# Base rows stored from SP instead of ACT, and 125-row transfers cut into 112 and 13 rows

## The chip, the cores and the metric

The kernel runs on one core of a Trainium2 chip. The metric is the device time of one execution in microseconds, as the median of repeated runs. The profile is of one further execution; its instruction span starts at the first instruction and ends at the last.

## What is computed

The reference is two layers of a graph network over 1,250 nodes with 512 features: graph convolutions over 21,250 edges, linear attention, and expert layers. Only its two ends matter here. At the very start the input is normalised row by row. At the very end stands a feed-forward layer with a shared part and two banks of eight experts, in which each row goes to one expert of each bank:

```python
xn = _layernorm(x, axis=-1)          # start of layer 0
...
shared = gelu(x2 @ Ws1 + bs1) @ Ws2 + bs2
y = shared
y = y + _bank_residual(x2, Wr_sp, br_sp, W1_sp, b1_sp, W2_sp, b2_sp)
y = y + _bank_residual(x2, Wr_fq, br_fq, W1_fq, b1_fq, W2_fq, b2_fq)
```

`_bank_residual` picks the likeliest expert for each row, sends the row through that expert's two matrices with a gelu between them, and scales the result by the gate. The gelu and the second product are as in `shared`. The result is added to `x`.

## The kernel before

The 1,250 rows are held as 10 tiles of 125 rows (`TP`), one row on one partition. `GROUPS` are the tiles 0 to 3, 4 to 7, and 8 and 9. `R1t` and `R2t` are two SBUF buffers of [125, 10, 512] floats.

**Start.** SP loads the indices `dst` and `src`, then group 0 of the input (`load_x(0)`, 125 rows of 8 KB, L2800), the first weight unit (L2841) and groups 1 and 2. DVE first works out edge bounds (to L2454). Then `x_stats(0)` waits for group 0 and takes its statistics (L2465). On these depend the normalised rows, all later stages and the loading of the next weight unit.

**Last expert of layer 0** (in `stream_dve`, L1794 to L1806). DVE adds the results of tiles to `R2t` (`down`: L1462 is the addition, which frees a PSUM bank, L1420 the statistics) and splits transposed columns (`low_cols`, L1457). Products `q` of TensorE (L630 to L632) follow. They need the columns of their group and a free bank; the order of banks is that of the list `MIX`, eight in a ring.

**Routing and shared part of layer 1.** ACT normalises rows of the three groups (L1110), stores each group to the DRAM tensor `d_xg` (`store_rows`, L1351), and interleaves this with head rows (L1357). From `d_xg` rows are later gathered for each expert tile. The shared part ends in ten products (L1042 to L1047). DVE adds each to `R2t` (`add_shared`, L2141) and raises `base_ready`. These ten tiles are the base rows of the output. ACT stores them to `out` at the end of `stream_act`, one transfer of 125 rows of 2 KB for each tile (L1416), and each one waits for its tile.

**Expert tiles.** Rows are placed in 34 tiles of 128 slots (`NS` = 17 for each bank). For tile q POOL gathers rows from `d_xg` (`fetch_rows`, L2969), TensorE transposes them (`rows_to_cols`, L3023), ACT copies them (`turned`, L3096), TensorE makes the hidden layer (`hidden`, L3036), ACT applies the gelu (L3104), TensorE multiplies by the second matrix (`expert_out`, L3058), DVE scales (L3161) and copies the first matrix of the tile q + 3 out of the bank (`fetch_w1`, L3151), and POOL adds the rows to `out` (L2986, accumulating indirect transfer). TensorE goes round in this order: transposes of q + 2, hidden layer of q + 1, output of q. Before the first of them it makes `bias_columns` (L3046), which ACT copies (L3109).

ACT runs its program in order: L3109 and all `turned` and `gelu` copies stand behind the ten stores of L1416. POOL is in order too: it issues the gathers of tiles 0 to 6, waits until all base rows are stored (`out_stored`), adds tile 0, 1 and 2, gathers tile 7, adds tile 3, gathers tile 8, and so on. The gathers of tiles 4 and up wait for the transposes of the tile four before.

**Weights of the two banks.** SP loads each bank in four transfers of 2,048 KB (`load_bank`, L2848). Those of bank 1 are the second half: the first two wait for the last hidden product of the shared part, the other two for the last use of the shared weights. Bank 1 is first read for tile 17.

Of the kernel before, what the change touches and what calls it, by code (L numbers as in the profile page):

```python
# [19 lines left out]
TP = 125  # L20
NT = N // TP
# [96 lines left out]
PER = 10  # L118
EARLY = 4
LAST_TURN = [4, 5, 4]  # L120
COUNT_PARTS = [(0, 640), (640, 960), (960, 1120), (1120, 1200), (1200, 1240), (1240, N)]

LAST_U, LAST_D = f"u{E0 - 1}", f"d{E0 - 1}"
# [48 lines left out]
def program(nc, A, out):  # L172
    ctx = ExitStack()
    with ctx:
# [3 lines left out]
        def sem(name):  # L178
            return ctx.enter_context(nc.semaphore(name))


        d_xg = nc.dram_tensor("d_xg", [N, D], F32).ap()
# [49 lines left out]
        R1t = R1[0:TP, :].rearrange("p (t d) -> p t d", t=NT)  # L232
        R2t = R2[0:TP, :].rearrange("p (t d) -> p t d", t=NT)
# [219 lines left out]
        x_in = [sem(f"x_in{i}") for i in range(3)]  # L453
# [24 lines left out]
        out_stored = sem("out_stored")  # L478
# [69 lines left out]
        rows_stored = sem("rows_stored")  # L548
# [16 lines left out]
        base_ready = sem("base_ready")  # L565
# [9 lines left out]
        def rows_normed(eng, site, t):  # L575
            eng.wait_ge(normed_rows, NT * (site - (site > 1)) + t)
# [8 lines left out]
        def mx_bank(name):  # L585
            return ps[:, MJ[name] % 8, :]
# [5 lines left out]
        def mx_evacuated(eng, name):  # L592
            eng.wait_ge(mx_free[MJ[name] % 8], MJ[name] // 8 + 1)
# [4 lines left out]
        def stream_pe(pe, n, unit, unit_done):  # L598
# [128 lines left out]
            rows_unit("wr0")  # L727
            pe.wait_ge(counts_rounded, NT - 1 + len(COUNT_PARTS))
            pe.wait_ge(heavy_ready, 1)
# [338 lines left out]
        def stream_act(act):  # L1068
# [85 lines left out]
            for g in range(3):  # L1154
                root(1, g)
            for i in range(NT - 1 + len(COUNT_PARTS)):
                t = min(i, NT - 1)
                a, b = COUNT_PARTS[i - t] if t == NT - 1 else (0, N)
                if i:
                    act.wait_ge(counts_rounded, i)  # L1160
                act.activation(CTr[0:TP, t, a:b], CT[:, t, a:b], ACT.Copy).then_inc(counts_rounded, 1)
            for g in range(3):
                t0, t1 = GROUPS[g][0], GROUPS[g][-1] + 1
# [184 lines left out]
            def store_rows(g):  # L1348
                t0, t1 = GROUPS[g][0], GROUPS[g][-1] + 1
                rows_normed(act, 7, t1)  # L1350
                act.dma_start(d_xg.rearrange("(t p) d -> p t d", p=TP)[:, t0:t1, :], R1t[:, t0:t1, :])\  # L1351
                    .then_inc(rows_stored, 16)

            def head_rows(*tiles):
                for t in tiles:
# [46 lines left out]
            for i in range(6):  # L1402
# [8 lines left out]
                    .then_inc(mx_sem(("su", i)), 1)  # L1411
                mx_evacuated(act, ("su", i))
                act.activation(HH[:, i % 2, c0:c0 + w], V[:, i % 4, 0:w], ACT.Copy).then_inc(shared_high, 1)
            for t in range(NT):
                act.wait_ge(base_ready, t + 1)
                act.dma_start(out[TP * t:TP * t + TP, :], R2t[:, t, :]).then_inc(out_stored, 16)  # L1416

        def stream_dve(dve, n, own, settle, row, heads, per_head, fetch_w1):
            def stats(src, t):
# [33 lines left out]
            def low_cols(site, name, ts):  # L1453
                for t in ts:
                    s = slice(TP * t, TP * t + TP)
                    dve.wait_ge(cols_high, NT * site + t + 1)
                    dve.tensor_tensor(XL[:, :, s], mx_bank((name, t))[:, 0:TP * KC].rearrange("p (k e) -> p k e", k=KC),  # L1457
                                      XH[:, :, s].bitcast(F32), ALU.subtract).then_inc(mx_sem((name, t)), 1)
# [288 lines left out]
            for e in range(E0):  # L1747
                def gelu_low(i):
                    c0, w = CH[i // 2]
                    v0, v1 = V[:, 2 * (i % 2), 0:w], V[:, 2 * (i % 2) + 1, 0:w]  # L1750
                    dve.wait_ge(gelu_ready, 12 * e + 2 * i + 2)
                    dve.tensor_tensor(v0, v0, v1, ALU.add).then_inc(gelu_summed, 1)
                    dve.wait_ge(hidden_high, 6 + 6 * e + i + 1)
                    dve.tensor_tensor(HL[:, i % 2, c0:c0 + w], v0, HH[:, i % 2, c0:c0 + w].bitcast(F32), ALU.subtract)\
                        .then_inc(hidden_low, 1)

                def up(i):
                    c0, w = CH[i // 2]
                    o = mx_wait(dve, (f"u{e}", i))
                    if e == 0:  # L1760
                        mx_evacuated(dve, ("wb", 2 * (i // 2) + 1))
                        mx_evacuated(dve, ("wb", 2 * (i // 2)))
                    dve.wait_ge(hidden_low, 6 + 6 * e + i - 1)
                    own(dve.tensor_tensor(V[:, 2 * (i % 2), 0:w], o[:, 0:w], BC[:, 0, c0:c0 + w], ALU.mult))
                    dve.tensor_tensor(V[:, 2 * (i % 2) + 1, 0:w], o[:, 0:w], BC[:, 1, c0:c0 + w], ALU.mult)\
                        .then_inc(mx_sem((f"u{e}", i)), 1)

                def down(some):
                    for t in some:
                        if e:  # L1770
                            mx_evacuated(dve, (f"d{e - 1}", t))
                        add_row((f"d{e}", t), R2t[:, t, :], R2t[:, t, :])
                        if e == E0 - 1:
                            mx_evacuated(dve, (f"d{e}", t))
                            stats(R2t[:, t, :], t)

                up(0)
                for i in range(1, 4):
                    up(i)
                    gelu_low(i - 1)  # L1780
                if e == E0 - 1:
                    gelu_low(3)
                    down(GROUPS[0])
                    spreads(0)
                    up(4)
                else:
                    up(4)
                    gelu_low(3)
                up(5)
                gelu_low(4)  # L1790
                gelu_low(5)
                if e < E0 - 1:
                    down(range(NT))
                else:  # L1794
                    scales(5, 0)
                    down(range(4, 6))
                    low_cols(5, "t6", GROUPS[0])
                    down(range(6, 8))
                    spreads(1)
                    down(range(8, 9))  # L1800
                    scales(5, 1)
                    down(range(9, 10))
                    spreads(2)
                    scales(5, 2)
                    low_cols(5, "t6", GROUPS[1])
                    low_cols(5, "t6", GROUPS[2])  # L1806
# [292 lines left out]
            for i, (c0, w) in enumerate(CH):  # L2099
                dve.wait_ge(shared_high, 4 + i)  # L2100
                dve.tensor_tensor(mT[PARTS:2 * PARTS, c0:c0 + w], mx_bank(("mt", i))[PARTS:2 * PARTS, 0:w],
                                  mT[PARTS:2 * PARTS, c0:c0 + w].bitcast(F32), ALU.subtract).then_inc(mx_sem(("mt", i)), 1)
            dve.wait_ge(rows_stored, 48)
            own(dve.tensor_scalar(tile_i, sloti[0:TP, :], 7, None, ALU.logical_shift_right))
            settle()
            own(dve.tensor_copy(tile_f, tile_i))
# [62 lines left out]
        def graph_pe(pe, n, unit, unit_done, v4):  # L2169
# [177 lines left out]
            for i in range(3):  # L2347
                turn_part(NG - 1, i, LAST_TURN[i])

        def graph_dve(dve, n, own, settle, row):  # L2350
# [109 lines left out]
                dve.tensor_tensor(wL[unit_slot(u)], wraw, wH[unit_slot(u)].bitcast(F32), ALU.subtract).then_inc(w_ready, 1)  # L2460

            def x_stats(g):
                dve.wait_ge(x_in[g], 16)
                for t in GROUPS[g]:
                    own(dve.bn_stats(bnst[0:TP, 6 * t:6 * t + 6], R1t[:, t, :]))  # L2465

# [118 lines left out]
            for b in range(NB):  # L2585
# [16 lines left out]
                if b - 1 in IN_LOOP:  # L2602
                    kind, t = IN_LOOP[b - 1]
# [53 lines left out]
        def graph_act(act, n):  # L2657
# [134 lines left out]
            for i in range(3):  # L2792
                store_turned(NG - 1, i, LAST_TURN[i])


        @block.sync
        def _(sp):
            def load_x(g):
                t0, t1 = GROUPS[g][0], GROUPS[g][-1] + 1
                sp.dma_start(R1t[:, t0:t1, :], A["x"][:, t0:t1, :]).then_inc(x_in[g], 16)  # L2800

            sp.dma_start(V[0:TP, 1, 0:NCH].bitcast(I32), A["dst"]).then_inc(edges_loaded, 16)
            sp.dma_start(V[0:TP, 0, 0:NCH].bitcast(I32), A["src"]).then_inc(edges_loaded, 16)
# [42 lines left out]
            def load_bank(g, e):  # L2846
                u = len(UNITS) + E * g + e
                sp.dma_start(wbank[g][:, UNIT * e:UNIT * e + 2 * UNIT].rearrange("p (e w) -> p e w", e=2),  # L2848
                             A["units"][u:u + 2].rearrange("e p w -> p e w")).then_inc(bank_loaded[g], 16)
# [5 lines left out]
            load_bank(0, 4)  # L2855
            sp.wait_ge(w_used, len(UNITS) - 1)
            load_bank(0, 6)
            sp.wait_ge(mx_full, MJ[("su", 5)] + 1)
            for e in (0, 2):
                load_bank(1, e)  # L2860
# [5 lines left out]
        def _(pool):  # L2866
# [50 lines left out]
            for u in range(EARLY, len(UNITS)):  # L2917
# [13 lines left out]
                if u == 4:  # L2931
                    pool.wait_ge(zeroed, 16)
                    pool.wait_ge(heavy_idx_ready, 1)
                    for t in range(NT):
                        pool.indirect_dma_start(
                            out=d_heavy, out_offset=bass.IndirectOffsetOnAxis(ap=heavy_idx[:, t:t + 1], axis=0),
# [34 lines left out]
                    in_offset=bass.IndirectOffsetOnAxis(ap=backi[:, q:q + 1], axis=0), bounds_check=N - 1, oob_is_err=False)\  # L2971
                    .then_inc(row_loaded[q % 4], 16)

            pool.wait_ge(rows_stored, 48)
            for q in range(4):
                fetch_rows(q)
            for q in range(2 * NS):
                if q == NS:
                    for i in range(3):
                        pool.wait_ge(y_added[i], 16 * len(range(i, NS, 3)))  # L2980
                for f in range(4, 7) if q == 0 else range(q + 4, min(q + 5, 2 * NS)) if q >= 3 else ():
                    fetch_rows(f)
                if q == 0:
                    pool.wait_ge(out_stored, 16 * NT)
                pool.wait_ge(y_ready, q + 1)
                pool.indirect_dma_start(  # L2986
                    out=out, out_offset=bass.IndirectOffsetOnAxis(ap=backi[:, q:q + 1], axis=0),
                    in_=ysb[q % 3], in_offset=None, bounds_check=N - 1, oob_is_err=False, compute_op=ALU.add)\
                    .then_inc(y_added[q % 3], 16)
# [243 lines left out]
```

## Time and profile before

| | |
|---|---|
| median of 3 runs | 1701.74 us (1699.98 to 1703.64) |
| profiled execution | 1704.72 us |
| its span of instructions | 1703.0 us |
| mean granted TensorE clock | 0.969 of full speed |
| TensorE busy | 1554.8 us (91%) |
| VectorE (DVE) busy | 989.0 us (58%) |
| ScalarE (ACT) busy | 445.3 us (26%) |
| GpSimd (POOL) busy | 305.7 us (18%) |

Busy time is that in which an engine carries out an instruction; waits and the issuing of transfers don't count in it. An engine name with a q (ACTq, SPq, POOLq, DVEq) is the queue or sequencer of this engine: there an issue of a transfer shows. The profiled execution lies 3.0 us above the median, and 1.7 us of it lie around the span.

### The profile page before, as it was taken

How to read it: one execution, taken by the hardware profiler on the slowest of the kernel's cores; microseconds unless marked ns; L12 is line 12 of the kernel's file. 1: busy time of each engine (PE TensorE's matmuls, PEld its weight loads, DVE VectorE, ACT ScalarE, POOL GpSimd, SP SyncE). 2: the span in 40 equal slices, each digit the busy share in tenths (PEclk: the TensorE clock that was granted, in tenths of full speed). 3: DMA queues.
4: the chain of work that ended last, by engine and by line, in shares of the span. 5: the costliest groups of instructions: out<-in, count | busy, mean ns of one | idle time of the engine just before them, and what ended most of it. 6: DMA issues, size and time to landing. Idle time of an engine off the chain costs nothing.

```text
span 1703.0 us, 23777 instructions
## 1 busy us (share of the span) xinstructions
PE 1554.8 (91%) x8983; PEld 1215.1 (71%) x8983; DVE 989.0 (58%) x1767; ACT 445.3 (26%) x854; POOL 305.7 (18%) x191
## 2 busy tenths in 40 slices
PE   3798887797999999999998999998999999896998
PEld 3677777786777777877786788877767755575765
DVE  6877778789954672386256666765254512762332
ACT  3422111123311220130124242434224101441222
POOL 1000002044111031004001212122111100002665
PEclk9899998999999999999998999999999999897999
DMA  4122224341221010012001010100101321545443
GB/s 148 49 66 88 96 94 151 128 149 63 86 92 49 1 66 28 1 49 68 25 1 50 25 50 26 50 26 25 50 25 51 115 87 68 222 166 186 67 80 45
DMA packets 51754, 123.93 MB, mean 73 GB/s; under 512 B 8033, under 2 KB 28408, under 8 KB 44510
## 3 DMA queue, kind: packets, MB, share of 16 engines
q1 hardware_dynamic: 12414, 62.78, 10.4%
q10 hardware_dynamic: 29375, 49.37, 8.3%
q0 software_dynamic: 9856, 10.28, 3.6%
q8 instruction: 74, 1.21, 0.3%
q14 instruction: 35, 0.29, 0.0%
HBM read 92.87 MB, written 40.22 MB: 78 GB/s over the span
## 4 chain that ended last, share of the span: by engine, by line
PE 75%; DVE 10%; DMA 7%; ACT 3%; issue 3%; ACTq 1%; POOL 1%; DVEq 0%; SPq 0%; POOLq 0%
PE ps L619 9%; PE ps L620 9%; PE ps L621 9%; PE ps L2284 5%; PE ps L677 4%; PE ps L679 4%; PE ps L630 4%; PE ps L631 4%; PE ps L632 4%; PE ps L938 3%; DMA arena<-d_kv 3%; PE ps L3036 3%; PE ps L3058 3%; PE ps L825 2%; DMA arena<-d_w 2%
## 5 line engine op out<-in xcount | busy, mean ns | idle before, releaser
L619 PE MATMUL ps<-wslot,XH 128*125 128x512 f32 (+2 forms) x560 | 215.0, 384 | 5.6 <-DVE XL L1457 3.9
L620 PE MATMUL ps<-wslot,XH 128*125 128x512 f32 (+2 forms) x560 | 212.9, 380 | 0.0
L621 PE MATMUL ps<-wslot,XL 128*125 128x512 f32 (+2 forms) x560 | 212.5, 380 | 0.0
L2927 POOL CAST wslot<-arena 128x2048 fp32r<-128x2048 f32 x25 | 47.7, 1907 | 798.2 <-PEq L3004 428.5
L630 PE MATMUL ps<-XH,wslot 128*128 128x500 f32 (+1 forms) x336 | 123.2, 367 | 16.2 <-DVE XL L1457 6.2
L1462 DVE TENSOR_TENSOR arena<-ps,arena 125x512 f32<-125x512 f32 x150 | 98.3, 684 | 50.5 <-PE ps L621 45.5
L619 PEld LDWEIGHTS ps<-wslot,XH 128*125 128x125 f32 x560 | 104.7, 187 | 31.4 <-issue 4.5
L677 PE MATMUL ps<-CTr,Hhi 125*128 125x500 f32 (+1 forms) x360 | 125.0, 361 | 0.0
L631 PE MATMUL ps<-XH,wslot 128*128 128x500 f32 (+1 forms) x336 | 121.6, 362 | 0.0
L621 PEld LDWEIGHTS ps<-wslot,XL 128*125 128x125 f32 x560 | 104.7, 187 | 22.8
L632 PE MATMUL ps<-XL,wslot 128*128 128x500 f32 (+1 forms) x336 | 120.8, 360 | 0.0
L620 PEld LDWEIGHTS ps<-wslot,XH 128*125 128x125 f32 x560 | 104.7, 187 | 21.9 <-issue 0.2
L2284 PE MATMUL ps<-arena 125*128 x1330 | 95.9, 228 | 26.2 <-DVE arena L2558 22.4
L2929 POOL TENSOR_TENSOR wslot<-arena,wslot 128x2048 fp32r<-128x2048 f32 x25 | 117.1, 4684 | 2.0
L679 PE MATMUL ps<-CTr,Hlo_head 125*128 125x500 f32 (+1 forms) x324 | 109.8, 352 | 0.0
L2284 PEld LDWEIGHTS ps<-arena 125*128 125x128 bf16 x1330 | 83.2, 102 | 33.7 <-issue 33.5
L2558 DVE TENSOR_SCALAR arena<-arena 125x1280 bf16<-125x1280 int16 x133 | 72.5, 570 | 47.0 <-PE ps L2284 46.3
L630 PEld LDWEIGHTS ps<-XH,wslot 128*128 128x128 f32 x336 | 65.7, 195 | 30.4 <-issue 17.3
L938 PE MATMUL ps<-arena 125*128 125x500 f32 (+1 forms) x240 | 84.6, 513 | 1.3 <-DMA arena<-d_w 1.3
L1511 DVE TENSOR_TENSOR V<-ps,BC 128x500 f32<-128x500 f32 (+1 forms) x36 | 21.3, 592 | 107.4 <-PE ps L683 106.6
L3036 PE MATMUL ps<-V,arena 128*128 128x128 f32 x544 | 69.5, 283 | 14.9 <-ACT V L3096 13.8
L677 PEld LDWEIGHTS ps<-CTr,Hhi 125*128 125x128 f32 x360 | 67.8, 188 | 15.1 <-issue 5.6
(445 smaller groups left out, 3062.6 us busy)
## 6 DMA issues: line engine op xcount, KB each, us to landing
arena<-in_units SPq DMA_DIRECT2D x29, 1024.0 KB, 4.8
arena<-in_units SPq DMA_DIRECT2D x8, 2048.0 KB, 11.1
d_w<-arena ACTq DMA_DIRECT2D x10, 625.0 KB
d_wt<-arena ACTq DMA_DIRECT2D x10, 625.0 KB, 3.5
rows<-in_rows ACTq DMA_DIRECT2D x22, 256.0 KB, 4.2
d_kv<-V SPq DMA_DIRECT2D x20, 250.0 KB
arena<-d_kv SPq DMA_DIRECT2D x20, 250.0 KB
arena<-d_wt ACTq DMA_DIRECT2D x2, 2441.4 KB
```

What stands on the lines that cost most here:

```text
L619: pe.matmul(o, lhsT=xh[:, k, s], rhs=H4[:, k, 0:nw], start=k == 0, stop=False, skip_group_check=True)
L620: pe.matmul(o, lhsT=xh[:, k, s], rhs=L4[:, k, 0:nw], start=False, stop=False, skip_group_check=True)
L621: last = pe.matmul(o, lhsT=xl[:, k, s], rhs=H4[:, k, 0:nw], start=False, stop=k == K - 1, skip_group_check=True)
L630: pe.matmul(o, lhsT=H4[:, k, f], rhs=XH[:, k, c0:c0 + w], start=k == 0, stop=False, skip_group_check=True)
L631: pe.matmul(o, lhsT=L4[:, k, f], rhs=XH[:, k, c0:c0 + w], start=False, stop=False, skip_group_check=True)
L632: last = pe.matmul(o, lhsT=H4[:, k, f], rhs=XL[:, k, c0:c0 + w], start=False, stop=k == KC - 1, skip_group_check=True)
L677: pe.matmul(o, lhsT=Hhi[0:TP, t, f], rhs=CTr[0:TP, t, c0:c0 + w], start=t == 0, stop=False, skip_group_check=True)
L679: pe.matmul(o, lhsT=Hlo[t][0:TP, f], rhs=CTr[0:TP, t, c0:c0 + w], start=False, stop=False, skip_group_check=True)
L938: last = pe.matmul(o, lhsT=src[:, t, 128 * m:128 * m + 128], rhs=slab_of(i)[:, t, 0:w], start=t == 0, stop=t == NT - 1, skip_group_check=True)
L2284: last = pe.matmul(ps[:, 3 * (b % 2) + t // 4, 128 * (t % 4):128 * (t % 4) + 128], lhsT=buffer[:, 128 * t:128 * t + 128], rhs=pre_flat[:, ...
L2929: pool.tensor_tensor(wL[unit_slot(u)], wraw, wH[unit_slot(u)].bitcast(F32), ALU.subtract).then_inc(w_ready, 1)
L3036: last = pe.matmul(ps[:, 2 + q % 2, ST * m:ST * m + ST], lhsT=w1_of[q][:, k // 2, FF * (k % 2) + 128 * m:FF * (k % 2) + 128 * m + 128], rh ...
```

## The change

The ten stores of base rows leave ACT's program. SP issues them, behind its loads of bank 0 and ahead of those of bank 1. Each transfer of 125 rows among the input loads, the stores to `d_xg` and the base rows becomes two, of rows 0 to 111 and 112 to 124, and the waits count twice as much. In the last expert of layer 0 the additions of tiles 6 and 7 stand ahead of `low_cols` of group 0 and their statistics behind it.

```diff
+ROW_PARTS = ((0, 112), (112, TP))
...
             def store_rows(g):
                 t0, t1 = GROUPS[g][0], GROUPS[g][-1] + 1
                 rows_normed(act, 7, t1)
-                act.dma_start(d_xg.rearrange("(t p) d -> p t d", p=TP)[:, t0:t1, :], R1t[:, t0:t1, :])\
-                    .then_inc(rows_stored, 16)
+                for a, b in ROW_PARTS:
+                    act.dma_start(d_xg.rearrange("(t p) d -> p t d", p=TP)[a:b, t0:t1, :], R1t[a:b, t0:t1, :])\
+                        .then_inc(rows_stored, 16)
...
-            for t in range(NT):
-                act.wait_ge(base_ready, t + 1)
-                act.dma_start(out[TP * t:TP * t + TP, :], R2t[:, t, :]).then_inc(out_stored, 16)
...
                     scales(5, 0)
                     down(range(4, 6))
+                    for t in (6, 7):
+                        mx_evacuated(dve, (f"d{e - 1}", t))
+                        add_row((f"d{e}", t), R2t[:, t, :], R2t[:, t, :])
                     low_cols(5, "t6", GROUPS[0])
-                    down(range(6, 8))
+                    for t in (6, 7):
+                        mx_evacuated(dve, (f"d{e}", t))
+                        stats(R2t[:, t, :], t)
                     spreads(1)
...
-            dve.wait_ge(rows_stored, 48)
+            dve.wait_ge(rows_stored, 96)
...
-                dve.wait_ge(x_in[g], 16)
+                dve.wait_ge(x_in[g], 32)
...
-                sp.dma_start(R1t[:, t0:t1, :], A["x"][:, t0:t1, :]).then_inc(x_in[g], 16)
+                for a, b in ROW_PARTS:
+                    sp.dma_start(R1t[a:b, t0:t1, :], A["x"][a:b, t0:t1, :]).then_inc(x_in[g], 16)
...
             load_bank(0, 6)
+            for t in range(NT):
+                sp.wait_ge(base_ready, t + 1)
+                for a, b in ROW_PARTS:
+                    sp.dma_start(out[TP * t + a:TP * t + b, :], R2t[a:b, t, :]).then_inc(out_stored, 16)
             sp.wait_ge(mx_full, MJ[("su", 5)] + 1)
             for e in (0, 2):
                 load_bank(1, e)
...
-            pool.wait_ge(rows_stored, 48)
+            pool.wait_ge(rows_stored, 96)
...
-                    pool.wait_ge(out_stored, 16 * NT)
+                    pool.wait_ge(out_stored, 32 * NT)
```

## Rows read from the trace of the kernel before

**Rows 1.** The page: the chain that ended last, by engine.

```profile
PE 75%; DVE 10%; DMA 7%; ACT 3%; issue 3%; ACTq 1%; POOL 1%; DVEq 0%; SPq 0%; POOLq 0%
```

**Rows 2.** The chain from 1537 to 1563 us: start us, us, what.

```profile
1539.15 9.21 ACTq L1416
...
1548.41 4.54 ACTq L1416
...
1553.76 3.78 PE ps L3036 x16
1557.55 0.85 PE ps L3023 x4
1558.40 2.42 PE ps L3036 x16
1560.82 1.72 PE ps L3058 x4
```

**Rows 3.** ACT's timeline, 1515 to 1555 us: start us, us, instruction [idle before].

```profile
1517.14 0.41 ACT L1413 ACTIVATE HH<-V 128x250 fp32r<-128x250 f32 x1
1523.87 29.08 ACTq L1416 DMA_DIRECT2D out<-arena  x10
1553.00 0.23 ACT L3109 ACTIVATE V<-ps 128x68 f32<-128x68 f32 x1 [35.44 <-issue]
```

**Rows 4.** TensorE's timeline ahead of its stop, 1539 to 1542 us.

```profile
1539.27 0.92 PE L3046 MATMUL ps<-BC,rows 8*128 8x17 f32 x7 [1.97 <-issue]
...
1540.24 1.09 PE L3023 MATMUL ps<-ident,rows 128*128 128x128 f32 x8
```

**Rows 5.** The chain some tiles later, at full clock.

```profile
1591.61 0.44 PE ps L3023 x4
1592.19 2.02 PE ps L3036 x16
...
1596.37 1.79 PE ps L3036 x16
```

**Rows 6.** Windows: busy of PE, PEld, DVE, ACT, POOL, granted clock, DMA share, GB/s.

```profile
1153.00:1157.00 4.00, 4.00 (x12) 3.20 (x12) 3.71 (x12) 0.30 (x1) 0.75 (x1) 0.57 0.54 176
1534.00:1538.00 4.00, 3.30 (x15) 2.32 (x13) 1.59 (x3) 0.00 (x0) 0.00 (x0) 1.00 0.32 126
1544.00:1548.00 4.00, 0.00 (x0) 0.00 (x0) 0.00 (x0) 0.00 (x0) 0.00 (x0) 0.50 1.02 422
```

**Rows 7.** The gather of tile 4, and the time to landing of all 34 gathers.

```profile
1541.66 1.00 POOL L2969 DMA_INDIRECT rows<-d_xg,BC  x1 [10.80 <-PE ps L3023]
...
DMA to landing us min/median/max: 2.9/3.9/8.1
```

**Rows 8.** The chain at the gather of tile 7.

```profile
1574.32 4.31 DMA rows<-d_xg,BC
```

**Rows 9.** SP's issues of bank loads (L2848) in ns, and their time to landing.

```profile
L2848 SPq DMA_DIRECT2D arena<-in_units x8: 367/376/480, 1449.6 to 1537.8; - x8
...
DMA to landing us min/median/max: 7.3/11.1/17.2
```

**Rows 10.** DVE's timeline at the start; the second row is of 0 to 28 us.

```profile
11.07 0.69 DVE L2454 TENSOR_SCALAR BC<-BC 128x40 f32<-128x40 f32 x4
15.02 2.47 DVE L2465 BATCH_NORM_STATS2 small<-arena 125x6 f32<-125x512 f32 x4 [3.25 <-DMA arena<-in_x]
```

**Rows 11.** The chain at ACT's stores of normalised rows.

```profile
1476.50 0.26 ACTq L1351
1476.76 0.33 issue
...
1486.78 0.26 ACTq L1351
```

**Rows 12.** DVE's timeline in the last expert of layer 0.

```profile
1149.63 2.43 DVE L1457 TENSOR_TENSOR XL<-ps,XH 128x500 fp32r<-128x500 f32 x4 [0.57 <-ACT XH L1083]
1151.98 0.68 DVE L1462 TENSOR_TENSOR arena<-ps,arena 125x512 f32<-125x512 f32 x1
```

**Rows 13.** TensorE's timeline at the first product that follows.

```profile
1152.81 0.46 PE L630 MATMUL ps<-XH,wslot 128*128 128x500 f32 x1 [2.98 <-DVE arena L1462]
```

**Rows 14.** DVE's timeline: the copy of tile 17's first matrix, the first use of bank 1.

```profile
1621.66 0.69 DVE L3151 COPY arena<-arena 128x1024 f32 x1 [0.63 <-issue]
```

## The prediction

> **What bounds the kernel now.** I read the page first. The reader is to see there that the chain which ended last is three quarters TensorE and has only 1% in ACTq, ACT's issuing of transfers [rows 1]. An average over 1,700 us hides where that 1% lies, so I followed the chain through each place that the diff touches.
>
> At the end of the shared part the chain leaves TensorE altogether. It stands on L1416, ACT's stores of base rows, from 1539.15 to 1552.95 us, 9.21 and 4.54 us for two issues [rows 2]. ACT's own timeline shows the same from the other side: its last copy ends at 1517.6, the ten issues stretch over 29.08 us, and the next activation, L3109, comes at 1553.00 after 35.44 us without work [rows 3]. TensorE has done the bias columns and the transposes of two tiles by 1541.33 [rows 4] and then waits for ACT's copy until 1553.76. The last base row is ready when the chain enters ACTq at 1539.15, so what comes behind is the issuing itself. The windows say why an issue takes that long. From 1534 to 1538 us, with only the 125-row stores under way, the DMA share is 0.32 at 126 GB/s, while bank loads of 128 rows reach 1.02 and 422 GB/s in 1544 to 1548 [rows 6]. A 125-row transfer thus occupies five of the sixteen DMA engines. On these five the stores stand behind 4 MB of bank loads, and ACT's issues are held up when too much is outstanding. That last link is inferred from the order of events; the stall is measured.
>
> **The stores move to SP.** ACT loses ten issues, and L3109 stands directly behind a copy that ends at 1517.6. The next thing that is late is TensorE itself. Its bias columns and transposes don't move: they follow the last base addition. They end at 1540.24 + 1.09 = 1541.33 [rows 4]. ACT's copy of the first tile runs beside the second tile's transposes, so the hidden layer of tile 0 can start at about 1541.5 instead of 1553.76. Behind that point the before needed 3.78 + 0.85 + 2.42 + 1.72 and small gaps, to 1562.54 [rows 2]. It had half the clock (0.50 in the window ahead [rows 6]) because TensorE had stood still. Without the stop these are 2.02 + 0.44 + 1.79 + 1.72 = 5.97 [rows 2, 5], so with 0.1 of gaps the output of tile 0 is full at 1547.6. That is 14.9 us earlier: 12.3 of wait and 2.6 of clock. Bounds: 12.3 if the clock falls as before, 15.0 if nothing else holds.
>
> SP gets twenty issues of at most 0.48 us [rows 9], two for each tile. An addition takes 0.68 us [rows 12], so SP may lag by one or two tiles, but the last ones wait for TensorE; it is through by about 1540.3. The DMA engines are empty at this time. At 422 GB/s a tile's 256 KB takes 0.6 us, and the fastest bank load landed 7.3 us after issue for 5.0 us of data at that rate, which leaves 2.3 us beside the data. All base rows are stored by about 1543.5, and POOL first asks for them when tile 0 is scaled, at about 1549. That wait costs nothing.
>
> What is queued behind the stores on SP are the four bank 1 loads. The first two start near 1540.5 instead of 1516.6. 8.39 MB plus some 1.5 MB of gathers and additions at 422 GB/s last until about 1564. Their first use is the copy for tile 17 at 1621.66 [rows 14], which moves to about 1608; 44 us of cover are left. The collision is elsewhere: gathers now run beside them. Beside bank loads a gather took up to 8.1 us, against a median of 3.9 [rows 7]. Tile 4's is issued at 1541.66 and lands by 1549.8, needed when tile 1's output is made, 1547.6 + 3.95 = 1551.6. Tiles 5 and 6 have more room. Tile 7's is issued behind POOL's addition of tile 2 and is on the chain already before, with 4.31 us at 1574.32 [rows 8]. Moved up by 14.9 it lies at 1559.4 to 1563.7, inside the loads. It then takes between 4.3 and 8.1 us, so it costs 0 to 3.8 us; I take the middle, 2.0. Later gathers find the queues empty. Net of this part: -14.9 + 2.0 = -12.9 us.
>
> **Input in 112 and 13 rows.** DVE is free at 11.76 and waits 3.25 us for group 0 of the input [rows 10]. Its 1,024,000 bytes take 8.1 us at 126 GB/s and 2.4 us at 422 [rows 6]. 112 rows divide over sixteen engines, and the remaining 13 rows are 106 KB. If the rate rises, the input lands at about 9.4 and the wait is gone: -3.25 us, which cannot be more since DVE's bounds come first. DVE's work behind it is the chain, so it carries on. The lower bound is 0. One issue more on SP ahead of the weight unit costs 0.4 us on a unit that isn't awaited before the statistics are done. In the Trainium skill, "DMA: Bandwidth & Descriptors", section "Why a DMA increments its semaphore by 16 and not by 1", the number of engines is the largest one up to 16 that divides the outer dimension: 5 for 125 rows, 16 for 112, 13 for 13. By that rule the trace agrees for 125 (0.32 is 5 of 16), and no row here shows the other two.
>
> **Normalised rows in two parts.** ACT issues three transfers more. An issue takes 0.26 and the next activation starts 0.30 to 0.59 after it [rows 11]. The first two are on the chain and the third nearly. I take 0.8 us, with bounds of 0.3 and 1.8. Their quicker landing wins nothing: DVE doesn't wait for `rows_stored` behind the routing.
>
> **The additions of tiles 6 and 7.** TensorE's first product starts at 1152.81, after the addition of tile 6, which starts at 1151.98 and lasts 0.68 [rows 12, 13]. With both additions first, DVE uses its 0.57 us of idle time, but `low_cols` starts some 0.7 us later and ends near 1152.75 instead of 1152.06, and the product needs that too. 0 us, with 0.5 either way.
>
> **Sum.** -12.9 - 3.25 + 0.8 = -15.35 us. The profiled execution took 1704.72, so its like would take 1689.4. It is 3.0 above the median of the runs. From the median, 1701.74 - 15.35 = 1686.4 us.
>
> **The rivals.**
> - *The clock falls all the same.* Between 1537 and 1541.5 TensorE has only small products and one pause of 1.97 us [rows 4]. After a pause of 2.98 us [rows 13] it got 0.57 of the clock for 4 us [rows 6], so 0.43 x 4 = 1.7 us were lost. Here: 1688.1. For it, the low use; against it, a shorter pause.
> - *Cutting transfers doesn't spread them.* The input still arrives at 15.0, and the base rows need about 20 us on five engines, until near 1546, still in time. 1686.4 + 3.25 = 1689.6. For it there is no row; against it, that 128-row loads use all engines. The Trainium skill, same page, section "Rules for kernel authors", says of two transfers to disjoint partition halves not to bother, since both go over the same engines; by that rule the result is this rival, but it speaks of a tile that divides evenly.
> - *Contention holds more than one gather.* If tiles 4 to 8 or the additions' landings each come late, I count two further delays of 3 us: 1692.4. Against it, POOL's slack of several us on tiles 5 and 6.
> - *ACT is not what holds tile 0.* Then only start and issues remain: -3.25 + 0.8, 1699.3, within 0.2%. Against it, gathers 0 to 3 and bank 0 have landed before 1541.
> - *Bank 1 comes too late* and the kernel is slower. Place: the copy for tile 17 at 1608. Each us of landing behind it costs one. It decides at 1608 + 15.35 = 1623, when the loads run below about 100 GB/s; at 90 GB/s they end near 1634 and the time is 1712. Against it stands 422 GB/s.
>
> **How the numbers follow.** The forecast has a chance of 0.60, the clock 0.17, no spreading 0.08, more contention 0.08, ACT not the cause 0.04, bank 1 0.03. Bounds of the forecast: tile 7's gather 2.0 less or 1.8 more, issues 0.5 less or 1.0 more, the reorder 0.5: 1683.4 to 1689.7. With the clock, the missing spread and the scatter of the runs (1.9) the range is 1682.5 to 1692. 0.2% (3.4 us) is about what this measurement can tell from no change. Faster by more than that: 0.60 + 0.17 + 0.08 + 0.08 = 0.93; same 0.04; slower 0.03.
>
> **What would show it.** L3109 directly behind `bias_columns`, near 1538 (with the start's shift); no pause of TensorE over 2 us between shared part and tile 0; clock 1.0 there; L2465 without a wait on `in_x`; a DMA share above 0.9 while the input loads; gather 7 landing in more than 4.3 us; bank 1 landing near 1562. I am wrong if TensorE's stop only finds another releaser, or if the 3.25 us come back as a wait between 20 and 80 us.

## The result, and the profile after

The changed kernel took 1696.09 us (median of 13 runs, 1691.34 to 1701.31) against 1703.68 us (13 runs, 1698.98 to 1710.93) for the kernel before: ratio 0.9952, 95% interval 0.9939 to 0.9966. It is faster, by 8 us where 15 were forecast, and its time lies above the predicted range. A later comparison gave 0.9959 (0.9942 to 0.9975). The ratios here and below are not the plain quotients of the medians; they differ from them by up to 0.0014. Single runs of one kernel spread over 10 us. The profiled execution took 1692.29 us, so the stages are compared below, not the ends.

The chain after, in the order of time (start us, us, what), over the stretch that answers to [rows 2] and [rows 8]:

```profile
1535.83 3.53 PE ps L3045 x16
1539.36 0.59 PE ps L3032 x4
1539.95 1.79 PE ps L3045 x16
1541.74 1.72 PE ps L3067 x4
...
1554.77 10.13 DMA rows<-d_xg,BC
1564.94 1.11 PE ps L3032 x4
1566.06 3.62 PE ps L3045 x16
1569.68 2.07 PE ps L3067 x4
```

ACTq is gone from it. In its place stands a wait that was 4.31 us before: the gather of tile 7, now 10.13 us. What follows runs slowly: 1.11, 3.62 and 2.07 us for the transposes, the hidden layer and the output product, which take 0.44, 1.79 and 1.72 at full clock.

ACT's timeline after, and below it SP's, which answer to [rows 3]:

```profile
1512.10 0.41 ACT L1415 ACTIVATE HH<-V 128x250 fp32r<-128x250 f32 x1
1534.59 0.23 ACT L3118 ACTIVATE V<-ps 128x68 f32<-128x68 f32 x1 [22.08 <-PE ps L3055]
```

```profile
1518.82 15.69 SPq L2866 DMA_DIRECT2D out<-arena  x20
1534.55 3.42 SPq L2853 DMA_DIRECT2D arena<-in_units  x4
```

ACT no longer waits in its queue but for TensorE's bias columns (L3055), and SP issues the four loads of bank 1 together, behind the last base row.

TensorE's timeline after:

```profile
1564.94 1.11 PE L3032 MATMUL ps<-ident,rows 128*128 128x128 f32 x4 [5.72 <-DMA rows<-d_xg,BC]
```

Windows after (columns as in [rows 6]):

```profile
1536.00:1540.00 4.00, 4.00 (x22) 4.00 (x23) 0.49 (x1) 0.81 (x4) 2.36 (x2) 0.57 0.89 330
1548.00:1552.00 4.00, 4.00 (x27) 3.00 (x26) 1.49 (x3) 1.28 (x4) 1.59 (x1) 1.00 1.00 400
1560.00:1564.00 4.00, 0.00 (x0) 0.00 (x0) 1.45 (x2) 0.00 (x0) 2.78 (x3) 0.93 1.02 280
1564.00:1568.00 4.00, 3.06 (x14) 2.82 (x15) 0.00 (x0) 0.60 (x1) 0.97 (x1) 0.50 0.81 165
```

The DMA engines are full until 1564. The granted clock falls twice: to a mean of 0.57 in the window of the hidden layer of tile 0, and to 0.50 after the stop at tile 7.

DVE's timeline at the start, which answers to [rows 10]:

```profile
11.17 0.69 DVE L2458 TENSOR_SCALAR BC<-BC 128x40 f32<-128x40 f32 x4
12.05 2.47 DVE L2469 BATCH_NORM_STATS2 small<-arena 125x6 f32<-125x512 f32 x4 [0.19 <-DMA arena<-in_x]
```

The wait for the input fell from 3.25 to 0.19 us.

Stages of each profiled execution, in us. A: start of the input statistics. B: from the first store of normalised rows to the transposes of the logits (the scores by which a row's expert is picked). C: from the first bias column to the first output product of tile 0. D: from there to the end. A, B and C are starts, or differences of starts, in the traces; D is the span less the start of that output product.

| kernel | A | B | C | D |
|---|---|---|---|---|
| before | 15.0 | 21.4 | 21.3 | 142.5 |
| after | 12.0 | 22.4 | 8.0 | 149.1 |
| change, second profile (d4) | 12.0 | 24.2 | 7.6 | 149.7 |
| a1, bank 1 left out | 12.0 | 22.4 | 7.9 | 143.4 |
| a2, half of bank 1 first | 12.1 | 24.0 | 7.7 | 142.1 |
| a3, gathers early | 11.9 | 22.9 | 8.0 | 141.0 |
| a4, bank 1 late | 13.3 | 23.9 | 7.6 | 152.1 |
| b1, input alone | 12.0 | 21.4 | 21.4 | 142.8 |
| b2, move alone | 15.2 | 21.3 | 6.3 | 152.9 |
| b3, cut stores on ACT | 15.0 | 21.3 | 7.5 | 143.4 |
| c1, a2 and a3 | 11.9 | 22.6 | 7.9 | 135.7 |
| d1, all on ACT, gathers early | 11.9 | 21.4 | 6.3 | 135.7 |
| d2, gathers early alone | 15.1 | 21.3 | 21.2 | 135.6 |
| d3, c1 with two parts undone | 11.9 | 21.4 | 6.4 | 135.7 |

### The profile page after: what moved, and what is told of

The parts are those of the page before. It is cut to its first block, busy times and chain, and to the rows that moved or that the text cites. A ratio compares the mean times of both kernels' runs of the same rounds, so it can differ in the third digit from the quotient of the medians.

```text
span 1690.6 us, 23793 instructions
## 1 busy us (share of the span) xinstructions
PE 1555.0 (92%) x8983; PEld 1214.2 (72%) x8983; DVE 989.6 (59%) x1767; ACT 445.7 (26%) x854; POOL 305.1 (18%) x191
## 4 chain that ended last, share of the span: by engine, by line
PE 75%; DVE 11%; DMA 5%; issue 3%; ACT 3%; POOL 1%; PEld 0%; DVEq 0%; ACTq 0%; PEldq 0%; SPq 0%; POOLq 0%
PE ps L620 9%; PE ps L621 9%; PE ps L622 9%; PE ps L2288 6%; PE ps L678 4%; PE ps L680 4%; PE ps L631 4%; PE ps L632 4%; PE ps L633 4%; PE ps L939 3%; PE ps L3045 3%; PE ps L3067 3%; PE ps L826 2%; DMA d_w<-arena 2%; DMA arena<-d_w 2%
## 5 line engine op out<-in xcount | busy, mean ns | idle before, releaser
L1510 DVE TENSOR_TENSOR V<-ps,BC 128x500 f32<-128x500 f32 (+1 forms) x36 | 21.3, 592 | 107.3 <-PE ps L684 106.6
L678 PEld LDWEIGHTS ps<-CTr,Hhi 125*128 125x128 f32 x360 | 67.8, 188 | 15.1 <-issue 5.6
L1129 ACT ACTIVATE V<-V,cols 128x500 f32<-128x500 f32 (+1 forms) x96 | 56.0, 631 | 85.1 <-DVE V L1764 85.1
```

Source lines behind the costliest of these rows:

```text
L678: pe.matmul(o, lhsT=Hhi[0:TP, t, f], rhs=CTr[0:TP, t, c0:c0 + w], start=t == 0, stop=False, skip_group_check=True)
```

## The experiments

The theory after the result: the loads of bank 1, late and all together, hold the gather of tile 7. It is tested by taking the loads away, moving them, and giving the gather more time.

**a1: bank 1 is not loaded**, and tiles 17 to 33 take bank 0's weights, so the second bank's weights are left out of the computation.

```diff
-            sp.wait_ge(mx_full, MJ[("su", 5)] + 1)
-            for e in (0, 2):
-                load_bank(1, e)
-            sp.wait_ge(w_used, len(UNITS))
-            for e in (4, 6):
-                load_bank(1, e)
...
```

> The changed kernel without the four loads of bank 1; tiles 17 to 33 take bank 0's weights instead, so the second bank's weights are left out. Theory (contention): tile 7's gather took 10.1 us beside these loads and stopped TensorE for 5.7 us, after which the clock was at half for a while. Without them it lands in about 4.3 us, TensorE waits under 1 us, and some 7 us are saved against the changed kernel: ratio to the kernel before 0.991, against 0.995 for the change itself. Rival A (the gather is late for another reason, such as the additions to rows that were just stored): TensorE still waits 5 us at tile 7, ratio 0.995. Rival B (the missing gain was lost before the expert tiles): tile 7 no longer waits, but the time hardly moves.

Measured: 1688.88 us, ratio 0.9923 (0.9897 to 0.9949). TensorE waited 2.1 us in all for gathers instead of 7.1, and D fell from 149.1 to 143.4. The loads are the cause of the late gather; rivals A and B fall.

**a2: the first two loads stand ahead of the base rows again.**

```diff
+            sp.wait_ge(mx_full, MJ[("su", 5)] + 1)
+            for e in (0, 2):
+                load_bank(1, e)
             for t in range(NT):
                 sp.wait_ge(base_ready, t + 1)
...
-            sp.wait_ge(mx_full, MJ[("su", 5)] + 1)
-            for e in (0, 2):
-                load_bank(1, e)
             sp.wait_ge(w_used, len(UNITS))
```

> The changed kernel with the first two loads of bank 1 ahead of the base rows on SP, as they were before the change; the other two behind. Theory (contention): 4 MB of the 8 are through before the shared part ends, the rest by about 12 us after its end, and tile 7's gather (some 21 us after it) finds empty queues: it lands in 4 to 5 us, TensorE waits under 1 us, ratio to before 0.991. The base rows stand behind 4 MB on SP's queue, but they are asked for only 12 us after the last of them. Rival A: the wait of 5 us at tile 7 stays, ratio 0.995. Rival C (base rows behind bank loads are late again): the addition of tile 0 waits for them, ratio above 0.995.

Measured: 1688.67 us, ratio 0.9902 (0.9877 to 0.9927). TensorE's waits for gathers sum to 0.6 us and D is 142.1, against 142.5 before the change. The whole loss in D came from the place of 4 MB of loads.

**a3: each gather from tile 7 on one addition earlier.**

```diff
-                for f in range(4, 7) if q == 0 else range(q + 4, min(q + 5, 2 * NS)) if q >= 3 else ():
+                for f in range(4, 7) if q == 0 else range(q + 5, min(q + 6, 2 * NS)) if q >= 2 else ():
```

> The changed kernel with each gather from tile 7 on issued one addition earlier (tile q + 5 ahead of the addition of tile q). Theory (contention, and no slack of the gathers): tile 7's is issued about 4 us earlier, still beside the loads, takes 8 to 10 us and stops TensorE for 1 to 2 us instead of 5.7; the small waits of later tiles (7.5 us in all by the trace after) vanish as well. Ratio to before 0.991 to 0.992. Rival A': POOL is the bound in the tiles and order makes no difference, ratio 0.995.

Measured: 1687.04 us, ratio 0.9903 (0.9878 to 0.9927), a little better than expected, though the stop itself was priced too low. The gather of tile 7 took longer still, 11.43 us where 8 to 10 were expected, and it had only the additions of tiles 0 and 1 ahead of it. The chain of a3:

```profile
1552.38 11.43 DMA rows<-d_xg,BC
```

TensorE stops for 3.2 us at this tile instead of 1 to 2, and never again for a gather: D is 141.0 with this stop in it.

**a4: bank 1 held back until six tiles are scaled.**

```diff
+            sp.wait_ge(y_ready, 6)
             sp.wait_ge(mx_full, MJ[("su", 5)] + 1)
```

> The changed kernel with all four loads of bank 1 held back until tile 5 is scaled. Theory (contention, any gather has next to no slack): tile 7's gather lands in about 4 us, but one issued beside the loads, of tile 10 or later, takes 8 to 10 us and stops TensorE for 4 to 6 us; ratio 0.994 to 0.995, as the change itself. Rival A (it is special to the first additions): no tile waits over 2 us, ratio 0.991.

Measured: 1699.1 us, ratio 0.998 (0.9965 to 0.9995), slower than the change itself. SP's issue and TensorE's stop, from the two timelines of a4:

```profile
1568.42 2.11 SPq L2853 DMA_DIRECT2D arena<-in_units  x4
```

```profile
1580.56 1.11 PE L3033 MATMUL ps<-ident,rows 128*128 128x128 f32 x4 [5.14 <-DMA rows<-d_xg,BC]
```

The stop moved with the loads, from tile 7 to tile 10, whose gather is the first one issued after them and takes 9.33 us (at 1571.18). D grew to 152.1, which is 3.0 more than in the change and more than expected. Another 1.3 us are lost at the start: in this trace alone of those with the cut input, the statistics begin at 13.3 instead of 12.0. So tile 7 is not special. The gather of tile 12 takes about 13.1 us (from 1579.04), but TensorE stands for it only 0.7 us: after one long stop the next gathers have slack.

The next four take the change apart.

**b1: the input loads alone.**

```diff
...
-                sp.dma_start(R1t[:, t0:t1, :], A["x"][:, t0:t1, :]).then_inc(x_in[g], 16)
+                for a, b in ((0, 112), (112, TP)):
+                    sp.dma_start(R1t[a:b, t0:t1, :], A["x"][a:b, t0:t1, :]).then_inc(x_in[g], 16)
```

> The kernel before with the input loads alone in 112 and 13 rows. Theory: DVE's wait of 3.25 us for group 0 of the input falls to 0.2 us as in the trace after, and all later work moves up by 3.0 us: ratio 0.998. Rival (the start's gain is given back by a later wait): DVE's wait is gone but the time doesn't move, ratio 1.000.

Measured: 1699.79 us, ratio 0.9983 (0.9968 to 0.9998), and A fell from 15.0 to 12.0. The time is as expected, so the gain at the start is carried to the end, though the interval only just excludes no gain at all.

**b2: the stores on SP, uncut.**

```diff
-            for t in range(NT):
-                act.wait_ge(base_ready, t + 1)
-                act.dma_start(out[TP * t:TP * t + TP, :], R2t[:, t, :]).then_inc(out_stored, 16)
...
+            for t in range(NT):
+                sp.wait_ge(base_ready, t + 1)
+                sp.dma_start(out[TP * t:TP * t + TP, :], R2t[:, t, :]).then_inc(out_stored, 16)
             sp.wait_ge(mx_full, MJ[("su", 5)] + 1)
```

> The kernel before with the base rows stored from SP at the new place, but each in one transfer of 125 rows, and nothing else changed. Theory: ACT is free, so TensorE's stop of 12.4 us ahead of tile 0 goes, as in the change. The ten stores need some 20 us on five engines and all four loads of bank 1 stand behind them on these engines, so they land later than in the change and hold tile 7's gather at least as long (over 5 us of wait): ratio 0.996 to 0.998. Rival (the cut into 112 and 13 rows is what helps at this place): TensorE still stops over 5 us before tile 0 or at the addition of tile 0.

Measured: 1699.22 us, ratio 0.9975 (0.9957 to 0.9994). C fell by 15.0 us, and D rose by 10.4. The queue and the stop, from the timelines of b2:

```profile
1537.09 7.75 SPq L2845 DMA_DIRECT2D arena<-in_units  x4
```

```profile
1550.56 1.64 POOL L2986 DMA_INDIRECT out<-arena,BC  x1 [7.97 <-DMA out<-arena]
...
1556.26 1.08 POOL L2969 DMA_INDIRECT rows<-d_xg,BC  x1 [0.30 <-issue]
```

```profile
1569.65 1.11 PE L3023 MATMUL ps<-ident,rows 128*128 128x128 f32 x4 [9.56 <-DMA rows<-d_xg,BC]
```

The slow stores hold SP's four issues of the loads for 7.75 us, and POOL's first addition waits until the stores have landed. The next two follow at once, so the gather of tile 7 is issued 20.2 us after the first bias column, no later than in the change (21.3). But it lands about 13.4 us later, where the change has 10.13, and stops TensorE for 9.56 us. So beside the move the cut saves 3 to 4 us of D. ACT is freed here without any cut: C is 6.3.

**b3: the stores cut, still on ACT.**

```diff
             for t in range(NT):
                 act.wait_ge(base_ready, t + 1)
-                act.dma_start(out[TP * t:TP * t + TP, :], R2t[:, t, :]).then_inc(out_stored, 16)
+                for a, b in ((0, 112), (112, TP)):
+                    act.dma_start(out[TP * t + a:TP * t + b, :], R2t[a:b, t, :]).then_inc(out_stored, 16)
...
```

> The kernel before with the base rows still stored by ACT, at the old place, but in transfers of 112 and 13 rows; nothing on SP moves. Theory: ACT was held because its 125-row stores pile up on five engines; over sixteen they are through in under 1 us each, the last issue ends about 1 us after the last base row, and TensorE's stop shrinks from 12.4 us to under 2. The loads of bank 1 keep their old place, so tile 7's gather isn't late: some 12 us are won, ratio 0.992 to 0.993, more than by the change itself. Rival (an issue from ACT is slow because it competes with SP's bank loads, whatever its shape): the stalls of 10 and 4.5 us in ACT's queue remain, ratio 0.998 to 1.000.

Measured: 1691.13 us, ratio 0.9911 (0.9886 to 0.9936). This is the run that tells most. ACT's timeline in b3:

```profile
1529.10 15.71 ACTq L1417 DMA_DIRECT2D out<-arena  x20
1545.03 0.23 ACT L3110 ACTIVATE V<-ps 128x68 f32<-128x68 f32 x1 [22.29 <-PE ps L3047]
```

The issues themselves, in ns (shortest, median, longest), before and in b3:

```profile
L1416 ACTq DMA_DIRECT2D out<-arena x10: 268/566/9972, 1523.9 to 1548.4; - x10
```

```profile
L1417 ACTq DMA_DIRECT2D out<-arena x20: 327/410/937, 1529.1 to 1544.3; - x20
```

Twenty issues take 15.71 us, the time in which the base rows come, where ten took 29.08 [rows 3]. None takes over 0.94 us, where the longest took 9.97. ACT's next activation waits for TensorE and not for the queue. The loads keep their old place, so D is 143.4. The cut alone, without a new engine, gives more than the whole change: what held ACT was the shape of the transfer, and b2 shows the same shape holding SP. An issue from ACT beside SP's bank loads is not slow in itself.

**c1: a2 and a3 together.**

```diff
+            sp.wait_ge(mx_full, MJ[("su", 5)] + 1)
+            for e in (0, 2):
+                load_bank(1, e)
             for t in range(NT):
                 sp.wait_ge(base_ready, t + 1)
...
-                for f in range(4, 7) if q == 0 else range(q + 4, min(q + 5, 2 * NS)) if q >= 3 else ():
+                for f in range(4, 7) if q == 0 else range(q + 5, min(q + 6, 2 * NS)) if q >= 2 else ():
```

> The changed kernel with both edits that won 8 us each: the first two loads of bank 1 ahead of the base rows, and the gathers one addition earlier. Theory: both take away the same wait, so they don't add: about 1 us more than either, from the small waits of later tiles; ratio 0.989 to 0.990. Rival (they take away different waits): 0.986 or less.

Measured: 1680.3 us, ratio 0.9854 (0.9829 to 0.9878). My theory that both take away the same wait falls; the rival's 0.986 is met. Windows of TensorE (busy, clock, DMA share, GB/s), before and in c1:

```profile
1600.00:1640.00 40.00, 38.29 (x236) 1.00 0.34 59
```

```profile
1600.00:1640.00 40.00, 40.00 (x243) 1.00 0.46 85
```

Far from any bank load the kernel before leaves TensorE idle for 1.7 us in 40. With early gathers it is never idle. D is 135.7, which is close to 34 rounds of 3.95 us (134.3).

**d2: early gathers on the kernel before** (the edit of a3 alone).

```diff
-                for f in range(4, 7) if q == 0 else range(q + 4, min(q + 5, 2 * NS)) if q >= 3 else ():
+                for f in range(4, 7) if q == 0 else range(q + 5, min(q + 6, 2 * NS)) if q >= 2 else ():
```

> The kernel before with the gathers one addition earlier and nothing else. Theory: without contention too, each gather has no slack, and small waits make 34 tiles take 142.5 us from the first output on where the two edits together took 135.7; the order of gathers alone gives 6 us of that: ratio 0.996 to 0.997, with ACT's stop of 13.75 us unchanged. Rival (the early gather only helps when it meets bank loads): tile stage as before, ratio 1.000.

Measured: 1697.9 us, ratio 0.9959 (0.994 to 0.9977), C as before and D 135.6. So the order of gathers has a gain of 6.9 us of its own in D.

**d1: input cut, base rows cut but on ACT, early gathers** (the edits of b1, b3 and a3 on the kernel before; the one of the base rows is shown).

```diff
...
-                act.dma_start(out[TP * t:TP * t + TP, :], R2t[:, t, :]).then_inc(out_stored, 16)
+                for a, b in ((0, 112), (112, TP)):
+                    act.dma_start(out[TP * t + a:TP * t + b, :], R2t[a:b, t, :]).then_inc(out_stored, 16)
...
```

> The kernel before with three edits that each won alone: input loads in 112 and 13 rows, base rows in 112 and 13 rows but still from ACT, gathers one addition earlier. SP's order, the stores of normalised rows and DVE's order stay as before. Theory: the base rows' shape is what freed ACT, their engine is of no matter, and the three gains are of three places and add: 15 + 3 + 6 us, ratio 0.985 to 0.986, as with the stores on SP behind half of bank 1. Rival (ACT's twenty issues cost time that SP's don't): 0.988 or more.

Measured: 1677.51 us, ratio 0.986 (0.9831 to 0.9889). The gains add as expected.

**d3: c1 without the cut of the normalised rows and with the old order of additions** (against c1; the stores are shown).

```diff
-                for a, b in ROW_PARTS:
-                    act.dma_start(d_xg.rearrange("(t p) d -> p t d", p=TP)[a:b, t0:t1, :], R1t[a:b, t0:t1, :])\
-                        .then_inc(rows_stored, 16)
+                act.dma_start(d_xg.rearrange("(t p) d -> p t d", p=TP)[:, t0:t1, :], R1t[:, t0:t1, :])\
+                    .then_inc(rows_stored, 16)
...
```

> The changed kernel with bank 1's first loads first and gathers early, and with two parts of the change undone: normalised rows are stored to DRAM in one transfer each (three issues fewer on ACT), and the additions of tiles 6 and 7 stand behind low_cols again. Theory: the three issues cost 0.3 us each on the chain, the order of additions nothing; 0.6 to 0.9 us faster than with them, in the stretch from ACT's first such issue to the products on the last group, ratio 0.985. Rival (the quicker stores of normalised rows were worth something): slower by 1 us or more, ratio 0.986 to 0.987.

Measured: 1676.59 us, ratio 0.9853 (0.9825 to 0.988). The ratio is that of c1, so the time does not tell them apart. The stage does: B is 21.4 us in d3. In seven traces without the cut it is 21.3 to 21.4, in seven with it 22.4 to 24.2, median 22.9. The three extra issues cost 1.0 us at least, 1.5 in the middle and 2.8 at most. The order of additions is worth nothing: TensorE's pause ahead of its product [rows 13] is 2.98 us before and in d3, and 3.01 after, there behind `low_cols`:

```profile
1146.38 0.46 PE L631 MATMUL ps<-XH,wslot 128*128 128x500 f32 x1 [3.01 <-DVE XL L1456]
```

By the ratios d1 and d3 are 24 to 25 us faster than the kernel before, and 17 to 18 faster than the change (d4). Which of the two is better these runs do not say.

**d4: the change again.**

> The changed kernel itself, on the same chip as the three others, for a second look at its gain. By the runs so far: ratio 0.995, a wait of 4 to 7 us of TensorE at the transposes of tile 7.

Measured: 1695.52 us, ratio 0.9959 (0.9942 to 0.9975); TensorE stopped for 6.3 us at tile 7.

## Why the prediction was wrong

| step | forecast | after | second profile |
|---|---|---|---|
| input in two parts (A) | -3.25 | -3.0 | -3.0 |
| three issues more on ACT (B) | +0.8 | +1.0 | +2.8 |
| order of additions | 0 | 0 | 0 |
| ACT free ahead of tile 0 (C) | -14.9 | -13.3 | -13.7 |
| gathers beside bank 1 (D) | +2.0 | +6.6 | +7.2 |
| sum | -15.35 | -8.7 | -6.7 |

The two sums bracket the measured -7.6 us of the medians, but single executions scatter more than that, so the agreement proves little. From the start of the statistics to the first bias column the ten traces with cut input take 1517.9 to 1527.8 us, and B accounts for at most 2.8 of these 9.9. The two profiled times differ by 12.4 us: 8.7 in the stages of the table and the rest outside them, which is within this scatter.

**The step that failed** is the price of tile 7's gather: "It then takes between 4.3 and 8.1 us, so it costs 0 to 3.8 us; I take the middle, 2.0." The place and the releaser of the collision were right, and it did fall inside the loads; the size was not right. The gather took 10.13 us, TensorE stood for 5.72 us, and the round after the stop took 6.80 us instead of 3.95, since the clock had fallen. The upper bound came from [rows 7], from gathers that met two bank loads and no additions. Here the gather had the additions of tiles 0 to 2 ahead of it in POOL's queue, and these were slow themselves: 10.3, 11.4 and 11.6 us to their landing. All 34 additions, before and after:

```profile
DMA to landing us min/median/max: 2.7/4.7/5.4
```

```profile
DMA to landing us min/median/max: 2.7/4.7/11.6
```

A largest value of before is no bound for a mix of transfers that before did not have. The loads also lasted longer than I had them. I had put 23.5 us from the first issue to the last landing, at a steady 422 GB/s. In the trace after they are issued from 1534.55 on and the last one, issued at 1537.4, lands 26.9 us later, at 1564.3, so it is 29.8 us; the windows above have 330 and 280 GB/s beside 400. All eight bank loads after:

```profile
DMA to landing us min/median/max: 7.3/11.8/26.9
```

That the additions ahead add to the gather's delay is inferred. For it: the gathers of tiles 4 to 6, issued beside the same four loads with no addition ahead, took 7.7, 8.1 and 7.2 us, within the bound, while those of tile 7 with additions ahead took 10.1, 10.7 (d4) and 11.4 (a3), and that of tile 10 in a4 9.3. Against it: the gather of tile 7 was also the last one to be issued well inside the loads, and it landed 0.6 us after the last of them. A gather at this place without additions ahead was not tried, so what share each has stays open; that the loads are the cause is shown by a1 and a2.

**The same step, second part.** The stop's cost in clock, 2.85 us in that one round, was not in the sum, though the same text had priced it at 1.7 us for another pause.

**The clock ahead of tile 0** was a rival with a chance of 0.17. It came true: C is 8.0 us, with 0.57 of the clock in its window, 3.53 for the hidden layer instead of 2.02. The wait in C went as forecast (12.2 us of 12.3); of the 2.6 us of clock only 1.1 came. Over eleven traces with ACT free, C is 6.3 or 6.4 in three and 7.5 to 8.0 in eight. A gain of 14.9 needs the rarer case; 13.3 was the likelier one. What decides between them is open. The three with 6.3 or 6.4 (b2, d1, d3) store the normalised rows uncut, but so does b3 with 7.5; the seven that cut them have 7.6 or more.

**The three issues more on ACT** were priced too low as well: 0.8 us with an upper bound of 1.8, where the seven traces have 1.0 to 2.8.

**Right**: ACTq as the cause of the stop, the ten issues' removal from the chain, the input (b1), that quicker landing of the normalised rows wins nothing, that the new order of additions is neutral, that bank 1 is in time. The input landed later than I worked out, at 12.0 us instead of 9.4, which 0.19 us of wait show.

**The rivals.** That cutting doesn't spread is refuted by b3: the same stores on the same queue stop holding ACT. Where the Trainium skill bears on this (DMA: Bandwidth & Descriptors), its section "Rules for kernel authors" says that two transfers to disjoint partition halves are not worth it. That does not hold here for 125 partitions, as the 15.71 us for twenty issues in b3 show against 29.08 for ten. The same page's section "Why a DMA increments its semaphore by 16 and not by 1" ties the number of engines to the partitions, and with that the runs agree: the DMA share is 0.32 with the 125-row stores alone [rows 6], and from 10 to 12 us, beside the input loads, it is 0.34 before and 0.95 with them cut. Contention was right in kind. It held three additions for 10.3 to 11.6 us, but only one gather long enough to stop TensorE for more than 1 us.

**What the change got wrong.** Either edit of the base rows frees ACT by itself, the move (b2, C 6.3) and the cut (b3, C 7.5). So the move was not needed, and it put the base rows ahead of loads that then met the gathers. Of the 13 us won in C it gave back 6.6 in D. This is shown by a2 and b3, each of which keeps C and has D as before.

## What to carry over

When an engine hangs in its own DMA issues, look at the shape of the transfers before moving them to another queue: 112 + 13 partitions in place of 125 was enough here (b3). When a large prefetch is pushed back, find what it meets at its new time; a transfer on the chain with no slack pays for it, and its price cannot be read from a trace in which the two never met. Give such a transfer slack by issuing it one step earlier in its queue: here this was worth 7 us even where nothing collided.

## What was not expected of the hardware

The loads of the input in 112 and 13 rows fill the DMA engines without the rate of bank loads. In the window from 10 to 12 us after the change the DMA share is 0.95 and the rate 234 GB/s, where bank loads reach 1.02 and 422 [rows 6]:

```profile
10.00:12.00 2.00, 0.03 (x1) 0.03 (x1) 1.75 (x11) 1.89 (x3) 0.00 (x0) 1.00 0.95 234
```

The kernel before has 0.34 and 139 GB/s there, so the share went up 2.8 times and the rate 1.7 times.

What lowers the rate is open. Nor do the runs say why the same bank loads cost 3.0 us more of D in a4, where they start later, among steady additions and gathers, than in the change.
